# Turning x in 32x32 squares on VectorE, and moving two weight chunks into FFN1, in a quantized AdaLN feed-forward kernel

## The reference, cut to what matters

```python
# x (4,1024,512), cond (4,256); 4096 tokens in all
x_mean = mean(x, axis=1)
fused  = concat([x, x_mean, cond, cond], -1)           # 1536 wide
rel    = relu(fused @ W + b)                           # W (1536, 512)
def quant_linear(x, w, b):                             # fake quantization
    s_in = max(x) / 255; xq = clip(round(x / s_in), 0, 255) * s_in      # one scale over all of x
    s_w  = max(abs(w), axis=1) / 127; wq = clip(round(w / s_w), -128, 127) * s_w   # per row of w
    return xq @ wq.T + round(b / (s_in * s_w)) * (s_in * s_w)
h   = relu(quant_linear(rel, w1, b1))                  # w1 (2048, 512)
out = x + quant_linear(h, w2, b2)                      # w2 (512, 2048)
```

## Time and profile before

| | before |
|---|---|
| three timed runs | 349.22, 350.07, 350.48 us |
| the profiled execution, its own time | 349.05 us |
| its span in the profile | 346.8 us |
| TensorE busy | 337.3 us, 97% |
| VectorE busy | 271.4 us, 78% |
| ScalarE busy | 155.7 us, 45% |
| GpSimd busy | 1.1 us |
| DMA | 74.90 MB, mean 216 GB/s |

### The profile page before, as it was taken

One profiled execution on the slowest core, in us unless ns is written; L12 is line 12 of the kernel. 1 busy time (PEld: TensorE's weight loads), 2 busy tenths in 40 slices (PEclk: granted clock), 3 DMA queues, 4 the chain that ended last, 5 costly groups with the idle time before them and its releaser, 6 DMA issues.

```text
span 346.8 us, 5358 instructions
## 1 busy us (share of the span) xinstructions
PE 337.3 (97%) x1645; PEld 196.2 (57%) x1645; DVE 271.4 (78%) x590; ACT 155.7 (45%) x263; POOL 1.1 (0%) x8
## 2 busy tenths in 40 slices
PE   6999999999999999999999999989999999999996
PEld 5788888888868544444444444434444444444444
DVE  1877668658684789999999999988486595685996
ACT  2635225325412499970000000038959559568800
POOL 1000000000000000000000000000000000000000
PEclk9999999999999999999999999999999999999999
DMA  7965998964432128886781030037984399977116
GB/s 247 404 214 171 325 326 241 285 188 177 121 60 41 21 122 363 346 347 287 323 335 60 0 121 0 0 121 289 402 341 183 133 412 424 361 241 227 78 60 242
DMA packets 29934, 74.90 MB, mean 216 GB/s; under 512 B 17864, under 2 KB 18144, under 8 KB 22496
## 3 DMA queue, kind: packets, MB, share of 16 engines
q1 hardware_dynamic: 29920, 74.73, 59.7%
HBM read 45.37 MB, written 25.17 MB: 203 GB/s over the span
## 4 chain that ended last, share of the span: by engine, by line
PE 90%; DVE 4%; issue 3%; DMA 2%; SPq 0%; ACT 0%; DVEq 0%
PE bank L480 28%; PE bank L436 26%; PE bank L360 25%; PE bank L501 4%; PE bank L348 4%; DMA x_in<-in_x_dram 2%; PE bank L453 1%; DVE hidden L781 1%; DVE x_lo L618 1%; PE bank L448 1%; PE bank L399 1%; DVE steps L842 0%; DVE cw_lo L656 0%; PE bank L418 0%; SPq L225 0%
## 5 line engine op out<-in xcount | busy, mean ns | idle before, releaser
L436 PE MATMUL bank<-pool_r,w_t 128*128 (+1 forms) x480 | 103.8, 379 | 0.0
L781 DVE TENSOR_SCALAR_CACHE_REDUCE hidden<-bank,qb,hmax 128x512 f32 x128 | 97.6, 808 | 5.3 <-DVE hidden L781 1.5
L576 ACT ACTIVATE steps<-hidden,s_quant 128x512 int16 (+1 forms) x124 | 76.8, 708 | 21.1 <-DVE w_t L809 11.2
L436 PEld LDWEIGHTS bank<-pool_r,w_t 128*128 128x128 bf16 x480 | 47.0, 98 | 56.6
L480 PE MATMUL bank<-w_t 128*128 128x512 bf16 x256 | 56.2, 379 | 0.9 <-DVE w_t L844 0.9
L360 PE MATMUL bank<-x_hi,cw_hi 128*128 128x512 f32 x128 | 51.0, 398 | 0.8 <-issue 0.5
L360 PE MATMUL bank<-x_hi,cw_lo 128*128 128x512 f32 x128 | 49.9, 390 | 0.0
L360 PE MATMUL bank<-x_lo,cw_hi 128*128 128x512 f32 x128 | 49.9, 390 | 0.0
L623 DVE TENSOR_SCALAR_CACHE_REDUCE hidden<-bank 128x512 f32 (+1 forms) x31 | 21.3, 689 | 27.9 <-PE bank L360 27.9
L480 PEld LDWEIGHTS bank<-w_t 128*128 128x128 bf16 x256 | 24.8, 98 | 31.7 <-DVE w_t L844 1.5
L480 PE MATMUL bank<-w_t,pool_q 128*128 128x512 bf16 x192 | 41.9, 379 | 0.0
(11 more groups left out here) (101 smaller groups left out, 244.7 us busy)
## 6 DMA issues: line engine op xcount, KB each, us to landing
hidden_spill<-hidden SPq DMA_DIRECT2D x16, 1024.0 KB, 3.9
hidden<-hidden_spill SPq DMA_DIRECT2D x16, 1024.0 KB, 7.7
pool_q<-in_L_ffn_w_dram SPq DMA_DIRECT2D x8, 1024.0 KB, 5.5
pool_r<-in_x_dram SPq DMA_DIRECT2D x8, 1024.0 KB, 5.6
x_in<-in_x_dram SPq DMA_DIRECT2D x7, 1024.0 KB, 5.6
out_dram<-pool_r SPq DMA_DIRECT2D x7, 1024.0 KB, 4.2
pool_r<-in_L_cond_W_dram SPq DMA_DIRECT2D x1, 2048.0 KB, 11.0
x_in<-in_x_dram SPq DMA_DIRECT2D x2, 512.0 KB, 5.4
```

The source lines that it names most:

```text
L436: mm = pe.matmul(bank[ft % BANKS][:, :], w1_t[:, ft, k, :], act_q[:, bass.ds(n * (KD * TB) + k * TB, TB)], start=(k == 0), stop=(k == KD - 1))
L576: ins = act.activation(steps[:, q % 2, f, :], hidden[:, bass.ds(slot * HB + ft * TB, TB)], ACT.Copy, scale=s_quant[:, ft:ft + 1])
L781: dve.tensor_scalar(hidden[:, bass.ds(slot * HB + ft * TB, TB)], bank[ft % BANKS][:, :], qb1[:, ft:ft + 1], hmax[:, ft:ft + 1], ALU.add, A ...
```

## The change

1. **x from block 2 on is turned by VectorE.** The DMA now brings x in squares: partition 32c + i gets, for each of 16 groups of 32 tokens, the 128 features of group c. A block is four DMAs of 32 partitions with runs of 512 bytes (`x_squares`). VectorE transposes all 32x32 squares of one k in one instruction with a stride of four elements on the reading side, into `x_t` in SBUF (`turn_x` on the VectorE side). ScalarE rounds from `x_t`. The subtraction to `x_lo` is on GpSimd. TensorE has no transposes left for blocks 2 to 7. Blocks 0 and 1 are still turned by TensorE. The rows of W and the tokens of a block are taken in another order that fits.
2. **Block 0 goes k by k.** All four output tiles have their own bank (`REL` is four banks), and the products of k = 0 for all tiles come first. x of block 0 is loaded in four pieces, and W's piece 0 and the small rows are loaded by ScalarE's queue.
3. **The chunks move.** Chunk n-1 of the weights is handled in block n, and the cast is on ScalarE. `EARLY` = 6 chunks are in the first stage. Chunks 6 and 7 are handled in FFN1: VectorE scales chunk 6 after block 0 and chunk 7 after block 2, ScalarE quantizes chunk 6 after `quantize_act(3)` and chunk 7 after `quantize_act(5)`, SP turns them after the spills of blocks 0 and 2.
4. **The scales of w2** go to HBM and back, broadcast to all partitions, in SP's queue after the spills of the first four blocks; L428 and L547 are gone. The division of b2 moves from after block 3 to after block 5.
5. The loops of the first stage and of `quantize_act` and `take_h` are written out.

```diff
-    x_blocks = x.rearrange("b s d -> (b s) d").rearrange("(n p j) d -> n p (j d)", p=P, j=TJ)
+    x_blocks = x.rearrange("b s d -> (b s) d").rearrange("(n j p) d -> n p j d", p=P, j=TJ)
+    x_squares = x.rearrange("b s d -> (b s) d").rearrange("(n q i) (c e) -> n c i q e", q=TQ, i=R, c=CG)
+    EARLY = NB - 2
-        REL = bank[4:6]
+        REL = bank[4:8]
@@ SP
+                for c in range(CG):
+                    sp.dma_start(x_in[c * R:(c + 1) * R, par, :].rearrange("i (q e) -> i q e", q=TQ),
+                                 x_squares[n, c, :, :, :]).then_inc(x_landed[par], 16)
...
+                if n % 2 == 0:
+                    turn_w(EARLY + n // 2)
+            sp.wait_ge(sw_ready, NB)
+            sp.dma_start(s2_row.rearrange("(c p) -> p c", p=P), sw2[:, :], allow_slow_non_contiguous=True
+                         ).then_inc(s2_out, 16)
+            sp.wait_ge(s2_out, 16)
+            sp.dma_start(s2_b[:, :], s2_row.partition_broadcast(P)).then_inc(s2_landed, 16)
@@ GpSimd
+            for n in range(2, NB):
+                for k in range(KD):
+                    pool.wait_ge(hi_ready, KD * n + k + 1)
+                    pool.tensor_tensor(x_lo[:, n % 2, k, :], x_t[:, k, :], x_hi[:, n % 2, k, :].bitcast(F32),
+                                       ALU.subtract).then_inc(lo_ready, 1)
@@ TensorE
+            for n in range(1, NB - 1):
+                for ot in range(KD):
+                    relation(n, ot)
@@ ScalarE
+            for n in range(NB - 1):
+                for k in range(KD):
+                    take_hi(n + 1, k)
+                if n > 0:
+                    quantize_w(n - 1)
...
+            for n in range(1, NB):
+                quantize_act(n)
+                if n == 3:
+                    act.wait_ge(first_act_ready, KD + 1)
+                    quantize_w(EARLY)
+                if n == 5:
+                    quantize_w(EARLY + 1)
@@ VectorE
+            def turn_x(n):
+                dve.wait_ge(x_landed[n % 2], 16 * (CG * (n // 2) + n % 2))
+                dve.wait_ge(rel_done, KD * (n - 1))
+                squares = x_in[:, n % 2, :].rearrange("p (q r k) -> p k q r", q=TQ, k=KD)
+                for k in range(KD):
+                    if n > 2:
+                        dve.wait_ge(lo_ready, KD * (n - 1) + k + 1)
+                    dve.transpose(x_t[:, k, :].rearrange("p (q i) -> p q i", i=R),
+                                  squares[:, k, :, :]).then_inc(x_turned, 1)
...
-            with dve.Fori(0, SLOTS) as slot:
+            for slot in range(SLOTS):
                 take_h(slot, slot, None)
+                if slot % 2 == 0:
+                    scale_w(EARLY + slot // 2)
```

The quantization of a chunk waits for its scales (`winv_ready`), and `scale_w(7)` stands behind `take_h` of block 2:

```diff
+            def quantize_w(c):
...
+                act.wait_ge(winv_ready, c + 1)
```

More of the change, by code:

```diff
@@ L215, in load_w @@
                 sp.dma_start(dst, src).then_inc(w_landed[par], 16)
[L217 to L236, removed]
+            for j in range(TJ):
+                sp.dma_start(x_in[:, 0, j * D:(j + 1) * D], x_blocks[0, :, j, :]).then_inc(x0_landed[j], 16)
+            for k in range(1, KD):
+                sp.dma_start(cw_in[:, k, :], cw_turned[0, :, k, :]).then_inc(cw_landed[k], 16)
+            sp.dma_start(x_in[:, 1, :].rearrange("p (j d) -> p j d", d=D), x_blocks[1]).then_inc(x_landed[1], 16)
             for par in range(2):
@@ L261, in _, with load_chunk @@
[L261 to L277, removed]
+            def load_chunk(c):
+                if c < KD:
+                    load_w(w1_chunks, c, c % 2)
+                else:
+                    load_w(w2_chunks, c - KD, c % 2)
@@ new lines, in _ @@
+            sp.dma_start(b2_b[:, :], b2.partition_broadcast(P)).then_inc(b2_landed, 16)
+            for n in range(SLOTS):
+                sp.wait_ge(spilled[n % 2], 16 + 16 * FQ * (n // 2))
+                for q in range(FQ):
+                    sp.wait_ge(h_taken, BANKS + FT * n + 4 * (q + 1))
+                    sp.dma_start(spill[n, :, q * 4 * TB:(q + 1) * 4 * TB],
+                                 hidden[:, n * HB + q * 4 * TB:n * HB + (q + 1) * 4 * TB]).then_inc(spilled[n % 2], 16)
+                if n % 2 == 0:
+                    turn_w(EARLY + n // 2)
@@ L341, in keep_warm, with turned_by_pe, product, relation @@
                     pe.matmul(free_bank[:, 0:moving.shape[-1]], ident_bf[:, :], moving, start=True, stop=True)
[L343 to L354, removed]
+            def turned_by_pe(n, j, k):
+                return pe.transpose(XT[k][:, j * P:(j + 1) * P],
+                                    x_in[:, n, j * D:(j + 1) * D].rearrange("p (r k) -> p k r", k=KD)[:, k, :],
+                                    ident[:, :])
+            def product(n, k, ot, w, v):
+                return pe.matmul(REL[ot][:, :], w[:, k, ot * P:(ot + 1) * P], v[:, n % 2, k, :],
+                                 start=(k == 0 and w is cw_hi and v is x_hi),
+                                 stop=(k == KD - 1 and w is cw_lo))
+            def relation(n, ot):
+                pe.wait_ge(rel_taken, KD * (n - 1) + ot + 1)
                 for k in range(KD):
@@ L464, in _ @@
             pe.wait_ge(h_taken, FT * (NB - 1) + BANKS + 11)
-            pe.wait_ge(w_turned, 16 * NB)
+            for par in range(2):
+                pe.wait_ge(w_turned[par], 16 * NB // 2)
             keep_warm(6, w2_t[:, 0, :], bank[2])
@@ new lines, in _ @@
+                                 bank[0][:, 0:CK * B].rearrange("p (k b) -> p k b", k=CK)))
+            step(dve.tensor_copy(condb_col[:, :], bank[0][:, CONDB_AT:CONDB_AT + KD]))
+            dve.tensor_copy(b1_col[:, :], bank[0][:, B1_AT:B1_AT + FT]).then_inc(cols_taken, 1)
+            take_relation(0, 0)
+            for k in range(KD):
+                take_lo(1, k)
+            for ot in range(1, KD):
+                take_relation(0, ot)
+            for n in range(1, NB - 1):
+                turn_x(n + 1)
+                take_relation(n, 0)
+                if n == NB - 2:
```

354 lines of the change are left out of this document (166 added, 188 removed).

## The result

| | before | after |
|---|---|---|
| timed runs, median | 350.27 us (349.22 to 350.95, four runs) | 354.9 us (352.43 to 355.49, four runs) |
| ratio after to before | | 1.0121, 95% interval 1.0065 to 1.0178 |
| the profiled execution's own time | 349.05 us | 354.31 us |
| its span | 346.8 us | 352.3 us |
| mean granted clock of TensorE | 1.00 | 0.979 |

The account below looks back on a forecast made before the run. TensorE's queue was taken to bound the kernel: -10.5 (transposes) - 3.3 (start) + 12.1 (FFN1) + 2.2 (restart) = +0.5 us, put on the median 349.65, gave 350.2 us; range 347.0 to 355.5.

Parts of the forecast that it names:

- the chance of slower: Whole kernel: slower than before by more than 0.3%, chance 0.42; faster 0.29, within 0.3% 0.29.
- the forecast itself: Whole kernel: 350.2 us, no change that can be measured, own range 348.4 to 352, chance 0.45.
- a transpose above 1.35 us: First stage: rival that VectorE bounds it because the strided transpose is slow; 355 us at 1.55 us each, chance 0.20.
- a late x: First stage: rival that x's 512-byte runs arrive late, stopping VectorE and then TensorE; 352.5 to 355 us, chance 0.08.
- Transposes off TensorE, -10.5: First stage: six of seven transpose rounds of 1.75 us leave TensorE's path, the other engines' shares staying hidden; -10.5 us.
- DMA, 0: First stage: x in 512-byte runs gives 10 to 12.7 us of DMA work per block; cost 0, upper end 5 us.
- The start, -3.3: Block 0: first product at 8.2 us, queue without holes from 8.5 against 11.8; -3.3 us, ends -4.2 and 0.
- FFN1, +12.1: FFN1: chunk 7 on ScalarE waits for VectorE's scales, delays block 7's activations, TensorE stands 11.65 us; +12.1, ends +11 and +13.5.
- Restart, +2.2: After TensorE's pause in FFN1: half pace for 0 to 6.5 us costs 0 to 3.2 us; +2.2 taken.
- the rival without a restart cost: After TensorE's pause in FFN1: the restart costs nothing, 348.0 us, chance 0.17.

Follow-up runs that it names:

- both edits: Chunk 7 quantized behind ScalarE's last block of FFN1 and the rest of W loaded in block 2, against the changed kernel: 336.91 us, ratio 0.965 to the kernel before.

## Why the prediction was near, and where it was off

350.2 us was predicted, 354.9 measured, in the range, and the chance of slower, 0.42, was the largest of the three. But the forecast itself was no change, and that was wrong. That the time lies in the range is in part luck: it is above the forecast's own range (348.4 to 352), and the range reached to 355.5 for a transpose above 1.35 us or a late x, and neither came. Point by point:

- *Transposes off TensorE, -10.5.* Right: 10.6 when put back. The transpose took 1.07 us where I took 0.8 and where 1.35 was the limit; GpSimd 1.30 where I took 1.3. The Trainium skill, "Vector Engine (DVE) Microarchitecture Reference", section on the SBUF access granule, gives a read that hops 4 KiB with every element 0.68 ns more per column (1.73 against 1.05); the runs give 0.39 us over 512 columns for the step of 16 bytes, 0.77 ns each, so they agree roughly, and the estimate of 0.9 us for the whole was 0.17 short.
- *DMA, 0.* Right for x: VectorE did not wait for x in the changed kernel. The share of 1.05 over 73 us is 11.4 us of work per block of 10.9, between the two estimates of 10 and 12.7.
- *The start, -3.3.* Too large. Without the pause the bias products would have begun at 88.18 instead of 100.27, 12.1 us earlier; less the 10.5, the start gave 1.6. No run tests the start by itself. The first product came at 9.19 instead of 8.2: the sum had all of x there at about 6.7, from the bytes that the kernel before had moved by then, and the fourth piece, issued at 2.1 and 5.7 us on its way, landed at 7.9. The remaining 0.7 was not taken apart.
- *A term that was missing, +4.6.* The wait of 3.04 us for the rest of W, 1.24 more for its products at a falling clock, and 0.3 behind it. This is the step of the prediction that failed: under "DMA" it asked only whether x would be late, and counted the loads of a block; it did not follow where the 2 MB load had gone in SP's queue. In the changed kernel it stands under `n == NB - 3`, SP's round 5. The experiment with the early load gave back 4.4.
- *FFN1, +12.1.* Right in mechanism and nearly in size: TensorE's pause was 10.86 us, with some 0.4 of short waits. It was less than 11.65 because chunk 7 took ScalarE 4.4 us (156.59 to 160.99) and not 5.0, and block 6 4.9 and not 5.15. VectorE's arrears were made good by the end, as worked out: TensorE waits for it once in FFN1, in the table of waits. With the restart FFN1 was forecast 14.3 longer and is 13.2.
- *Restart, +2.2.* Right: four us at the 1.2 GHz level, half of which, 2.0, is lost, and the rival without a restart cost is out. The size is partly luck, since the length of the slow stretch varies (see the last section). The rule of the Trainium skill ("TensorE: Matmul & The Clock Gate", section on the clock gate) that an idle TensorE falls to the lower level held in both pauses of the changed kernel; in one pause of 3.13 us of another version it did not.

So -10.5 - 1.6 + 4.6 + 13.2 - 0.2 = +5.5, as by the spans. With the missing term and 1.6 instead of 3.3 for the start the same sum would have been +6.8, and the forecast "slower".

## What to carry to other kernels

When work is moved into a stage with slack, look not at the engine's total but at the position: a wait for something that another engine makes late holds up everything behind it on the same queue, and here 12 us of idle ScalarE became 11 us of idle TensorE although both engines had room. Follow each transfer that changes its place in a DMA queue to the instruction that needs it, also when it is not what the change is about. And a pause of the matrix engine can be paid twice, once as itself and once at the lower clock, and the second part is not in proportion to the first.

## What the runs showed of the hardware that was not expected

- The clock did not fall in every pause of about 3 us. In the changed kernel (3.04 us), with chunk 7 last (2.81 us) and with its scales one block earlier (2.94 us) the bias products took 3.16, 3.35 and 3.27 us; in the version with chunk 7 between blocks 6 and 7 a pause of 3.13 us was followed by products at full pace, 1.92 us. After pauses of 10.86 and 5.96 us it was low for 4.0 and 5.3 us of work: the shorter pause was followed by the longer slow stretch. With the rest of W early the pause was 10.86 us again, and the slow stretch 4.8 us (165.27 to 170.1).
- The start differs from one execution to the next. Four transposes of block 0 took 0.69 us in the changed kernel and 1.06 in the profiled execution with both edits, which took 338.28 us where the other four took 336.6 to 337.3.
- Writing the 512 scales of w2, 2 KB in pieces of 4 bytes, to HBM took 12.4 us to land (15.0 with both edits). Nobody waited for it.
- Casting to bf16 on ScalarE took 1.91 us for 128x2048 from int8 and from uint8 alike; VectorE had done it in 1.22 us (L645).
